# Graph attention with a quantised feed-forward: roots taken straight from the variances, two tiles' chains interleaved, the table load first, and the first unit rounded by VectorE

## The reference

```python
def _layernorm(x, axis=-1, eps=1e-05):
    m = jnp.mean(x, axis=axis, keepdims=True)
    v = jnp.var(x, axis=axis, keepdims=True)
    return (x - m) / jnp.sqrt(v + eps)

# graph layer, N = 384, H = 16 heads of D = 64
q = x @ wq.T + bq ; k = x @ wk.T + bk ; v = x @ wv.T + bv
q2, k2, v2 = second projections (wiq, wik, wiv), split into heads
mask = -inf, softplus(w)[edge_type - 1] at [src, dst], w[3] added on the diagonal where empty
attn = softmax(q2 k2^T / 8 + mask) ; out = (attn v2) @ wo.T + bo

# feed-forward, I = 352
def _act_fake_quant(x, clip_factor):
    scale = jax.nn.sigmoid(clip_factor) * jnp.max(jnp.abs(x)) / QMAX
    return jnp.clip(_ste_round(x / scale), -QMAX - 1.0, QMAX) * scale
xq = _act_fake_quant(x, clip_x[0])
h = _act_fake_quant(jax.nn.silu(gate) * up, clip_down[0])     # weights quantised per row

x = x + graph(_layernorm(x)) ; x = x + ffn(_layernorm(x))
```

## Time and profile before

| | before |
|---|---|
| median of 3 runs | 343.31 us (341.02 to 343.48) |
| the profiled execution | 339.95 us |
| its span | 338.0 us |
| TensorE busy | 325.0 us, 96% |
| VectorE busy | 237.3 us, 70% |
| GpSimd busy | 191.6 us, 57% |
| ScalarE busy | 180.0 us, 53% |
| chain that ended last | 55% PE, 14% DMA, 10% issue, 10% POOL, 9% DVE, 1% ACT |

### The profile page before, as it was taken

The page is one execution under the profiler, slowest core; times in us unless marked ns, Lnnn a source line. Parts: engine busy times, 40 slices in busy tenths (PEclk is TensorE's granted clock), DMA queues, the critical chain, the costliest instruction groups (busy, mean ns, idle before and its releaser), DMA issues.

```text
span 338.0 us, 6003 instructions
## 1 busy us (share of the span) xinstructions
PE 325.0 (96%) x2086; PEld 297.2 (88%) x2086; DVE 237.3 (70%) x610; ACT 180.0 (53%) x338; POOL 191.6 (57%) x253
## 2 busy tenths in 40 slices
PE   5999999999999999989999999999999999999985
PEld 5899998788999999989999999999999878887744
DVE  4857888854066554269985979779797875598764
ACT  3733256474653333333356868677595865243533
POOL 6786656656686777687966393654727757000000
PEclk9999999999999999999999999999999999999999
DMA  7996345576234343761331231303113110000005
GB/s 259 375 405 254 124 146 163 195 231 186 64 116 133 126 125 126 251 206 64 124 105 72 77 124 62 126 0 127 63 64 124 63 65 0 2 0 0 2 0 188
DMA packets 16763, 41.71 MB, mean 123 GB/s; under 512 B 3440, under 2 KB 7392, under 8 KB 16736
## 3 DMA queue, kind: packets, MB, share of 16 engines
q1 hardware_dynamic: 13824, 38.87, 33.6%
q0 software_dynamic: 2064, 1.80, 2.0%
q10 hardware_dynamic: 848, 0.70, 0.6%
HBM read 37.99 MB, written 3.37 MB: 122 GB/s over the span
## 4 chain that ended last, share of the span: by engine, by line
PE 55%; DMA 14%; issue 10%; POOL 10%; DVE 9%; ACT 1%; POOLq 0%; DVEq 0%; ACTq 0%
PE PS L699 32%; DMA codes<-ecol,place 11%; POOL codes L406 7%; PE PS L856 5%; PE PS L844 5%; PE PS L832 4%; DMA scratch<-codes 2%; DVE scratch L1204 2%; POOL ring L389 1%; PE PS L1004 1%; DMA X<-in_x 1%; PE PS L1019 1%; DVE scratch L1203 1%; PE PS L768 1%; PE PS L758 1%
## 5 line engine op out<-in xcount | busy, mean ns | idle before, releaser
L389 POOL TENSOR_TENSOR ring<-stage,ring 128x256 fp32r<-128x256 f32 x128 | 98.6, 806 | 39.3 <-ACT ring L471 37.2
L699 PE MATMUL PS<-XT,ring 128*128 128x384 f32 x528 | 94.2, 336 | 1.8 <-DVE AT L1103 1.3
L699 PEld LDWEIGHTS PS<-XT,ring 128*128 128x128 f32 x528 | 91.4, 188 | 2.8 <-DVE AT L1103 1.9
L406 POOL DMA_INDIRECT codes<-ecol,place x51 | 58.5, 1148 | 26.2 <-issue 15.0
L471 ACT ACTIVATE ring<-stage 128x1024 fp32r<-128x1024 f32 x52 | 54.3, 1056 | 1.7 <-DMA stage<-in_weights 1.5
L571 ACT ACTIVATE scratch<-scratch,smx 128x384 f32<-128x384 f32 x48 | 29.0, 605 | 18.8 <-DVE smx L1226 18.8
L1141 DVE TENSOR_TENSOR ring<-stage,ring 128x1024 fp32r<-128x1024 f32 x20 | 24.5, 1226 | 18.1 <-issue 11.9
L699 PE MATMUL PS<-QT,ring 128*128 128x384 f32 x192 | 35.5, 338 | 0.0
L699 PE MATMUL PS<-AT,ring 128*128 128x384 f32 x192 | 35.2, 338 | 0.0
L699 PE MATMUL PS<-ring,AT 128*128 128x512 f32 x144 | 34.6, 394 | 0.0
L699 PEld LDWEIGHTS PS<-AT,ring 128*128 128x128 f32 x192 | 33.1, 188 | 1.5 <-issue 1.5
(11 more groups left out here) (209 smaller groups left out, 479.8 us busy)
## 6 DMA issues: line engine op xcount, KB each, us to landing
stage<-in_weights SPq DMA_DIRECT2D x56, 512.0 KB
V<-in_w_gate_up SPq DMA_DIRECT2D x4, 512.0 KB, 6.9
codes<-scratch SPq DMA_DIRECT2D x3, 576.0 KB, 13.5
scratch<-codes POOLq DMA_DIRECT2D x3, 576.0 KB, 6.6
X<-in_x SPq DMA_DIRECT2D x3, 512.0 KB, 5.0
out<-X SPq DMA_DIRECT2D x4, 384.0 KB, 2.7
scratch<-in_w_gate_up SPq DMA_DIRECT2D x2, 512.0 KB
V<-in_w_down SPq DMA_DIRECT2D x5, 176.0 KB, 5.9
```

The source lines that it names most:

```text
L389: ins = pool.tensor_tensor(ring[1][:, slot, piece], stage[:, slot % STAGE, piece], ring[0][:, slot, piece].bitcast(F32), ALU.subtract)
L406: pool.indirect_dma_start(codes[b].rearrange("(n a) -> n a", a=1), bass.IndirectOffsetOnAxis(ap=place[:, t:t + 1], axis=0), ecol[:, VAL, t ...
L699: ins = pe.matmul(outs, lhs[a], rhs[b], start=start and n == 0, stop=stop and n == 2, skip_group_check=True)
```

## The change

The root. ScalarE takes it straight from the variance with scale 0.25 and a bias tile eps (`root`). VectorE's variance term (`root_first`) then runs beside it. Behind Wo the same form is used, with the factor 0.25, which was absent there; the factor 2.0 of the weight scales goes in return.

The start. The table load and its activation stand ahead of ScalarE's five small DMAs, behind a wait for GpSimd's first constants. Tile 1's sums come out as a variance (ROOT_C = 32, 32² = 1024), its root follows on ScalarE at once, and tiles 1 and 2 have a chain each, written in alternation. The dummies are 38 and 24, not 42 and 36.

Behind Wo. The last minimum stands ahead of bn_aggr. nmean of tile 2 is made on VectorE, and tile 2's second half goes to ScalarE (y_last). Unit 0 is scaled, clipped and rounded by VectorE alone, in three instructions from PSUM; ScalarE takes units 1 to 5. The weight scales stand between VectorE's units 3 and 4.

```diff
@@ ScalarE, start
+            act.wait_ge(consts, 5)
+            chain.step(act.activation(rs[:, 6, :], kinds[:, 0:NT], ACT.Sqrt))
             act.dma_start(edges[:, :, :], edge_cols).then_inc(edges_in, 16)
...
-            chain.step(act.activation(rs[:, 4, :], kinds[:, 0:NT], ACT.Sqrt))
+            def root(var, m):
+                act.activation(rs[:, 1, m:m + 1], var, ACT.Sqrt, scale=0.25, bias=eps[:, 0:1]).then_inc(root_ready, 1)
             act.wait_ge(var_ready, 1)
-            act.activation(rs[:, 1, 0:1], rs[:, 0, 0:1], ACT.Sqrt).then_inc(root_ready, 1)
+            root(mv[:, 0, 1:2], 0)
...
+            act.wait_ge(sums_in, 1)
+            root(sums[:, 2:3], 1)
             act.wait_ge(var_ready, 2)
-            act.activation(rs[:, 1, 1:NT], rs[:, 0, 1:NT], ACT.Sqrt).then_inc(root_ready, 1)
+            root(mv[:, 2, 1:2], 2)
@@ ScalarE, behind Wo
+            act.wait_ge(mean_ready, NT)
+            act.activation(V2[:, NT - 1, HC:C], X[:, NT - 1, HC:C], ACT.Identity, scale=rs[:, 2, NT - 1:NT],
+                           bias=nmean[:, NT - 1:NT]).then_inc(y_last, 1)
             act.wait_ge(x_scaled, 1)
-            for hf in range(2):
-                for m in range(NT):
+            for u in range(1, 2 * NT):
@@ TensorE
-            keep_clock(42, spare_columns, 7)
+            keep_clock(38, spare_columns, 7)
...
-                    keep_clock(36, spare_columns, 7)
+                    keep_clock(24, spare_columns, 7)
...
-                            pe.wait_ge(t_ready, i + 2)
+                            pe.wait_ge(t_ready, i + 1)
@@ VectorE, start
+            def root_first(var, m):
+                chain.link(dve.tensor_scalar(rs[:, 0, m:m + 1], var, LN_EPS, 0.25, ALU.add, ALU.mult))
+            def root_turn(n, m):
+                dve.wait_ge(root_ready, n)
+                chain.link(dve.reciprocal(rs[:, 4, m:m + 1], rs[:, 1, m:m + 1]))
+            def root_next(m):
+                chain.link(dve.scalar_tensor_tensor(rs[:, 3, m:m + 1], rs[:, 4, m:m + 1], rs[:, 0, m:m + 1],
+                                                    rs[:, 1, m:m + 1], ALU.mult, ALU.add))
+            def root_last(m):
+                chain.link(dve.reciprocal(rs[:, 2, m:m + 1], rs[:, 3, m:m + 1]))
@@ VectorE, behind Wo
-                    if t < 2 * NT:
-                        chain.link(dve.tensor_reduce(low_to, X[:, m, cs], X_AXIS, ALU.min))
+                    chain.link(dve.tensor_reduce(low_to, X[:, m, cs], X_AXIS, ALU.min))
...
+            chain.step(dve.tensor_scalar(units[0], turned(0, 0), gmx[:, 11:12], QMAX, ALU.mult, ALU.min))
+            chain.step(dve.tensor_scalar(units[0], units[0], -QMAX - 1.0, MAGIC, ALU.max, ALU.add))
+            dve.tensor_scalar(xqT[:, 0:4, 0:P], units[0], MAGIC, None, ALU.subtract).then_inc(xq_ready, 1)
```

More of the change, by code:

```diff
@@ L637, in _ @@
             o_take(7, 1)
-            chain.step(act.activation(rs[:, 4, :], kinds[:, 0:NT], ACT.Sqrt))
+            chain.step(act.activation(rs[:, 6, :], kinds[:, 0:NT], ACT.Sqrt))
             for m in range(NT):
                 act.wait_ge(var_ready, 2 + m + 1)
-                act.activation(rs[:, 1, m:m + 1], rs[:, 0, m:m + 1], ACT.Sqrt).then_inc(root_ready, 1)
+                root(mv[:, m, 1:2], m)
                 if m < NT - 1:
+                    act.wait_ge(mean_ready, m + 1)
                     act.activation(V2[:, m, :], X[:, m, :], ACT.Identity, bias=nmean[:, m:m + 1]).then_inc(centred, 1)
@@ L647, in _ @@
                     act.activation(V2[:, m, :], V2[:, m, :], ACT.Copy, scale=rs[:, 2, m:m + 1]).then_inc(y_scaled, 1)
-            chain.step(act.activation(rs[:, 4, :], kinds[:, 0:NT], ACT.Silu))
+            chain.step(act.activation(rs[:, 6, :], kinds[:, 0:NT], ACT.Silu))
+            act.wait_ge(mean_ready, NT)
+            act.activation(V2[:, NT - 1, HC:C], X[:, NT - 1, HC:C], ACT.Identity, scale=rs[:, 2, NT - 1:NT],
+                           bias=nmean[:, NT - 1:NT]).then_inc(y_last, 1)
             act.wait_ge(x_scaled, 1)
-            for hf in range(2):
-                for m in range(NT):
-                    act.wait_ge(yt_full, 2 * m + hf + 1)
-                    act.activation(units[NT * hf + m], turned(hf, m), ACT.Copy, scale=gmx[:, 11:12]
-                                   ).then_inc(t_ready, 1)
+            for u in range(1, 2 * NT):
+                hf, m = u // NT, u % NT
+                act.wait_ge(yt_full, 2 * m + hf + 1)
+                act.activation(units[u], turned(hf, m), ACT.Copy, scale=gmx[:, 11:12]).then_inc(t_ready, 1)
             act.wait_ge(scales_ready, 1)
@@ L1051, in _ @@
             dve.sem_inc(proj_low, 2)
-            def moments(m):
-                dve.wait_ge(x_in[m], 16)
-                for g in range(2):
-                    chain.link(dve.bn_stats(stats[:, m, g, :], X[:, m, g * HC:(g + 1) * HC]))
-                chain.join()
-                chain.step(dve.bn_aggr(mv[:, m, :], stats[:, m, :, :].rearrange("p a b -> p (a b)")))
-                return dve.tensor_scalar(rs[:, 0, m:m + 1], mv[:, m, 1:2], LN_EPS, 0.25, ALU.add, ALU.mult)
+            def root_first(var, m):
[8 more added lines that the diff above has]
+                chain.link(dve.reciprocal(rs[:, 2, m:m + 1], rs[:, 3, m:m + 1]))
             def norm(m, cs=slice(0, C)):
@@ L1075, in _ @@
+            for g in range(2):
+                chain.link(dve.bn_stats(stats[:, 0, g, :], X[:, 0, g * HC:(g + 1) * HC]))
+            chain.join()
+            dve.bn_aggr(mv[:, 0, :], stats[:, 0, :, :].rearrange("p a b -> p (a b)")).then_inc(var_ready, 1)
+            dve.wait_ge(var_ready, 1)
+            root_first(mv[:, 0, 1:2], 0)
+            root_turn(1, 0)
+            chain.join()
+            root_next(0)
+            chain.join()
+            root_last(0)
+            chain.join()
             norm(0)
-            chain.link(moments(2))
+            dve.wait_ge(x_in[2], 16)
@@ L1078, in _ @@
+            for g in range(2):
+                chain.link(dve.bn_stats(stats[:, 2, g, :], X[:, 2, g * HC:(g + 1) * HC]))
             dve.wait_ge(sums_in, 1)
-            chain.link(dve.tensor_scalar(mv[:, 1, 0:1], sums[:, 1:2], -1.0, None, ALU.mult))
-            dve.tensor_scalar(rs[:, 0, 1:2], sums[:, 2:3], 0.25 / C, 0.25 * LN_EPS, ALU.mult, ALU.add).then_inc(var_ready, 1)
-            v, root, inv, two = (rs[:, c, 1:NT] for c in range(4))
-            dve.wait_ge(root_ready, 2)
-            chain.step(dve.reciprocal(inv, root))
@@ L1084, in _ @@
-            dve.wait_ge(var_ready, 2)
-            chain.step(dve.tensor_tensor(two, inv, v, ALU.mult))
-            chain.step(dve.tensor_tensor(two, two, root, ALU.add))
-            chain.step(dve.reciprocal(inv, two))
+            root_first(sums[:, 2:3], 1)
+            chain.link(dve.tensor_scalar(mv[:, 1, 0:1], sums[:, 1:2], -ROOT_C, None, ALU.mult))
+            chain.join()
+            dve.bn_aggr(mv[:, 2, :], stats[:, 2, :, :].rearrange("p a b -> p (a b)")).then_inc(var_ready, 1)
+            root_turn(2, 1)
@@ L1088, in _ @@
+            chain.join()
+            root_next(1)
+            dve.wait_ge(var_ready, 2)
+            root_first(mv[:, 2, 1:2], 2)
+            chain.join()
+            root_last(1)
+            root_turn(3, 2)
+            chain.join()
+            root_next(2)
             norm(1)
+            chain.join()
+            root_last(2)
+            chain.join()
             norm(2, slice(HC, C))
```

83 lines of the change are left out of this document (43 added, 40 removed).

## The result

The change makes the kernel slower by about 0.8%.

A forecast was written before the change was run, and what follows sets the result against it. GpSimd's scatters end last by about 1.3 us, TensorE's projections beside them, both fed by the start. Gains 0.45 (start) + 0.05 (behind Wo) = 0.5, against the median 343.31: 342.8, range 340.3 to 344.0.

The forecast's parts named there:

- What bounds the kernel: Whole kernel: GpSimd's scatters end last by about 1.3 us; a gain at the start reaches them and TensorE's projections.
- The bound of 1% around no change: Measured time: within 1% (3.4 us) of no change, chance 0.92; 0.04 faster, 0.04 slower.
- erow's landing: Start, ScalarE's small DMAs: issued 1.5 later, erow still lands 5.3 behind its issue; cost zero.
- Rival C: Start: erow 2.5 later, queued behind four weight chunks, or small operations at 0.2 pitch; no gain, 343.3; chance 0.12.
- The gain at the start: Tile 1's norm at 10.65 in place of 11.11, first XT block likewise earlier: gain 0.45, bounds 0.05 and 0.55.
- Rival B: Start: X tile 0 lands up to 0.37 earlier without edges and erow in front; 342.4; chance 0.12.
- The table load: Start, ScalarE: the load takes 1.28 with no further drain of about 1.38 behind it, against the Trainium skill.
- Behind Wo: From Wo's output to gate and up's second halves: gain 0.05, bounds 0 and 0.15.
- the first operation on PSUM: Behind Wo, VectorE's first of three operations on unit 0, 512 wide: 0.62, ceiling 0.7.
- Roots with scale and bias cost as before: ScalarE's roots: the new form with scale and bias tile takes no longer than the old.
- the cover: Behind Wo: ScalarE's load and tile 2's second half end at 312.7, ahead of the scale at about 312.8; no delay.
- Rival D: Start: fewer dummies leave TensorE idle about 0.97, its clock falls, costing 1.8; 344.6; chance 0.08.

The follow-up runs named there:

- the second execution: The changed kernel measured and profiled again with nothing altered; ratio to the kernel before 1.0056.
- the low part first: Changed kernel with GpSimd's first low part placed ahead of its edge arithmetic, not behind it; ratio to the kernel before 0.9994.

## Why the prediction was wrong

**What bounds the kernel: right.** "So what the start gains, both long paths gain" held with the sign reversed. The low part came 2.25 late for TensorE, the first scatter 2.2 late, the last way of the code lists back into SBUF began at 142.04 for 140.11, and the time rose by 2.8 ± 1.2 and 1.9 ± 1.2. The bound of 1% around no change, to which the forecast gave 0.92, held; the direction did not.

**The step that failed: erow's landing.** The prediction wrote "erow lands 5.3 behind its issue, and if that holds GpSimd's edge arithmetic [...] ends at about 12.35", and took it to hold, so that the load's new place stood at nothing in the sum. It cost 2.25 of TensorE's time: erow landed 7.8 behind its issue. The 5.3 was measured for a DMA issued 0.9 ahead of the first weight chunk (1.25 and 2.19), with only X and edges in front; 1.5 later erow goes out behind that chunk, and the weights cost it 2.1. The step's own rule, free up to 1.75 later and beyond 2.05 each 0.1 costs 0.1, would have given 1.95 for 4.0 later, close to the 2.25 seen. Beside it GpSimd's arithmetic took 4.72 for 4.25, and TensorE asked at 16.0 and not at the 15.7 of the forecast; these two take each other back but for 0.2.

**Rival C: the mechanism named, the size wrong.** It put erow at 2.5 later and the time at 343.3, "no gain". By the same rule 2.5 costs 0.45, the very gain; the real 4.0 costs 1.95 by it, and cost 2.25. The number 2.5 had no row under it, and no upper end was given. One was at hand in the rows: the window of 4.00 to 4.70 ran at 382 GB/s, and four chunks of 512 KB take 5.5 us at that rate. On top of the 1.5 of the issue that is 7.0 later, 4.95 by the rule. Had C's bound been worked out so, its time would have reached beyond 347 and its chance decided the sign.

**The gain at the start: the mechanism right, the size a little small.** Without the late erow, tile 1's norm stood at 10.47 (forecast 10.65, before 11.11) and XT at 12.68 (forecast 12.85). The 0.64 is more than the 0.45 and above its upper bound of 0.55; 0.04 of it is an earlier X tile 0 (4.65 for 4.69).

**Rival B happened too, and was given back in part.** bn_stats of tile 0 starts at 4.09 for 4.69 in the changed kernel, 0.60 earlier and more than the 0.37 that B had as the most. In that execution VectorE then waits 0.82 for X tile 2, so that the first XT block gains 0.29 where it gains 0.64 with the DMAs in front. I put the later landing of X tile 2 to the small DMAs beside it, which no run separates. In the second execution there is no such wait, and the block gains 1.11. The late low part swallows either.

**The table load: right.** In the changed kernel the load at 315.38 took 1.28 and the next activation began at 316.68. The Trainium skill (ScalarE: Activation LUTs, What ACT_TABLE_LOAD costs) gives a drain behind a load; the trace after disagrees as that of before did. The skill's warning pointed at the right edit for another reason than the real one.

**Behind Wo: +0.12 for −0.05.** The mis-sized term is the first operation on PSUM: it took 0.75 (taken: 0.62, the ceiling was 0.7). The estimate beside it, about 0.6, comes out only if 0.26 of fixed part is taken off twice the 0.43, and no row was named for that. With it unit 0's bits end 5.76 behind the addition where they ended 5.74 behind it, and the 0.15 that the units were to come earlier is gone. The scales between units 3 and 4 then cost the 0.14 that the forecast had for them, and unit 5 ends at 9.88 for 9.72; TensorE waits for it, as forecast, but later. "Roots with scale and bias cost as before" was wrong as well, 0.30 for 0.20 behind Wo, so that ScalarE's load comes 0.23 later and not 0.16, and tile 2's second half took 0.82 for 0.6; VectorE waits for ScalarE nowhere behind it, so the cover held all the same.

**Rival D:** it did not occur in the changed kernel, though TensorE idled 1.68 there and not the 0.97 of the forecast: the sixteen transposes took 1.97 as before. Its price, from the run without dummies, is half of that given. That its 344.6 is the measured median, 344.63, is chance: the mechanism is another, and the sum started from 343.31 where the larger sample of the kernel before has 342.13.

## What to carry to other kernels

A DMA moved back by 1.5 us need not land 1.5 later; here it landed 4.0 later. It shares the engines with what other queues put on their way in between, and its flight before does not give its flight then. When an edit delays small transfers past the start of a bulk load, price them from the bulk's bytes over the measured rate as the upper end, and follow what stands behind their first reader in that engine's queue: here the reader had some 2 us of slack, and the low parts behind it had 0.4. What needs early arrival goes out first, and a table load that is hidden anyway can wait.

## What the hardware showed that was not expected

- 56 KB in rows of 512 bytes took 5.3 us issued 0.9 ahead of the weights, 5.7 issued 1.5 later with the weights held back, and 7.8 issued then behind the first of four weight chunks (7.5 in a second execution).
- GpSimd's cast of 128x56 values took 0.71 beside VectorE's norm (L378 above, at 11.00 beside the norm at 10.82) and 0.23 away from it. The whole edge arithmetic took 3.94 with no norm beside it (the low part first), 4.25 before, with the norm at 7.47 beside it, and 4.72 in the changed kernel, with the norms of tiles 1 and 2. No run tests the cause, and the cast just ahead of L378 took 0.23 beside the same norm.
- TensorE's clock went down behind idles of 2.03, 2.34 and 2.51 us and stayed up behind 1.68, 2.25 and 2.68 in others. These lengths alone don't order the cases.
- A tensor_scalar of 128x512 fp32 from PSUM took 0.75 on VectorE, for 0.43 from SBUF. ScalarE's root of 128x1 took 0.29 to 0.30 with scale and bias tile, 0.20 without.
